# A gated cross-attention block on one core: the whole order of loads and stages replaced

## The reference

```python
x = x + tanh(g_xattn[0]) * fake_quant(layernorm(x)) @ fake_quant(ctx)       # 512 rows of 512, ctx (2, 512, 512)
x = x + tanh(g_ffn[0]) * (layernorm(x) @ W_base.T + b_base + 0.5 * low_rank_update(x))
q, k, v = layernorm(x) @ w_q.T, ctx @ w_k.T, ctx @ w_v.T                    # 32 heads of 16, 8 key/value groups
x = x + tanh(g_xattn[1]) * (softmax(mask(q @ k.T / 4)) @ v) @ w_out.T       # 256 queries, 512 keys, batch 2
h = weight_quant(w_gate), weight_quant(w_up), weight_quant(w_down)          # ternary weights, 1376 hidden
x = x + tanh(g_ffn[1]) * bitlinear(relu(bitlinear(n, w_gate))**2 * bitlinear(n, w_up), w_down)   # n = layernorm(x)
```

## Time and profile before

| what | value |
|---|---|
| median of 3 runs | 261.47 us (261.21 to 261.71) |
| span of the profiled execution | 259.9 us; its own whole time is not given, the runs lie 1.3 to 1.8 us above the span |
| TensorE matmul busy | 244.6 us (94%) |
| VectorE busy | 206.9 us (80%) |
| ScalarE busy | 190.2 us (73%) |
| GpSimd busy | 124.0 us (48%) |
| bytes moved | 27.63 MB |

### The profile page before, as it was taken

The page is one execution under the profiler, slowest core; times in us unless marked ns, Lnnn a source line. Parts: engine busy times, 40 slices in busy tenths (PEclk is TensorE's granted clock), DMA queues, the critical chain, the costliest instruction groups (busy, mean ns, idle before and its releaser), DMA issues.

```text
span 259.9 us, 4692 instructions
## 1 busy us (share of the span) xinstructions
PE 244.6 (94%) x1472; PEld 120.2 (46%) x1472; DVE 206.9 (80%) x592; ACT 190.2 (73%) x317; POOL 124.0 (48%) x176
## 2 busy tenths in 40 slices
PE   8488989799999999999999999999999999998984
PEld 8443449647433343474244365434334244444431
DVE  3789676669898479767999995989888974999995
ACT  3536598659798998587698388998969988546631
POOL 7005920466332207455888662558978987100000
PEclk9959999999999999999999999999999999999999
DMA  6999962660497850004500830720000000000004
GB/s 190 358 372 358 405 267 63 142 132 4 111 316 221 153 161 3 0 1 112 74 0 0 308 140 0 153 32 1 5 0 0 3 0 0 3 1 0 3 0 161
DMA packets 9154, 27.63 MB, mean 106 GB/s; under 512 B 1514, under 2 KB 4122, under 8 KB 7882
## 3 DMA queue, kind: packets, MB, share of 16 engines
q1 hardware_dynamic: 8698, 21.63, 28.9%
q0 software_dynamic: 288, 5.70, 6.3%
q10 hardware_dynamic: 144, 0.00, 0.0%
HBM read 23.87 MB, written 3.41 MB: 105 GB/s over the span
## 4 chain that ended last, share of the span: by engine, by line
PE 71%; DVE 7%; DMA 7%; SPq 6%; ACT 6%; issue 3%; DVEq 0%; ACTq 0%
PE bank L804 12%; PE bank L831 11%; PE bank L782 10%; DMA big<-in_ctxT 7%; PE bank L807 7%; PE bank L854 5%; PE bank L872 5%; PE bank L724 4%; PE bank L714 4%; PE bank L790 4%; PE bank L760 2%; PE bank L839 1%; DVE fs L1317 1%; SPq L470 1%; PE bank L749 1%
## 5 line engine op out<-in xcount | busy, mean ns | idle before, releaser
L1252 DVE CUSTOM_DVE_ANT_0 junk<-bank,maskb 128x512 bf16<-128x512 f32 x128 | 83.8, 687 | 13.5 <-PE bank L782 12.6
L1026 ACT ACTIVATE big<-bank 128x512 f32<-128x512 f32 x128 | 75.1, 596 | 15.1 <-PE bank L804 10.8
L590 POOL TENSOR_TENSOR big<-big,product 128x512 int32<-128x512 int32 x48 | 61.6, 1285 | 33.6 <-ACT big L1026 33.2
L804 PE MATMUL bank<-qst,kst 99*128 99x512 bf16 x128 | 49.0, 383 | 0.2
L782 PE MATMUL bank<-kst,qst 96*128 96x512 bf16 x128 | 47.8, 381 | 0.6 <-DVE mx L1252 0.4
L831 PE MATMUL bank<-big,vp 128*32 128x512 f32 x256 | 30.6, 598 | 0.0
L807 PE MATMUL bank<-ident_b,maskb 128*128 128x512 bf16 x80 | 30.4, 380 | 0.0
L600 POOL TENSOR_TENSOR mx<-mx 128x4 f32<-128x4 f32 x64 | 16.0, 249 | 22.0 <-DVE mx L1252 19.6
L782 PEld LDWEIGHTS bank<-kst,qst 96*128 96x128 bf16 x128 | 12.5, 99 | 21.4 <-issue 11.0
L804 PEld LDWEIGHTS bank<-qst,kst 99*128 99x128 bf16 x128 | 12.4, 97 | 20.6 <-ACT big L1026 7.2
L1009 ACT ACTIVATE qst<-bank 3x512 bf16<-3x512 f32 x32 | 18.9, 590 | 0.9
(11 more groups left out here) (190 smaller groups left out, 413.2 us busy)
## 6 DMA issues: line engine op xcount, KB each, us to landing
...
stage_w<-in_w_gate SPq DMA_DIRECT2D x1, 2752.0 KB, 15.7
stage_w<-in_w_up POOLq DMA_DIRECT2D x1, 2752.0 KB, 14.8
...
```

The costliest lines, as they stand in the source:

```text
L590: nc.gpsimd.tensor_tensor(p, p, keep[:, nt, KEEP_ST.index(i):KEEP_ST.index(i) + 1, :].broadcast_to([P, HG, P]), ALU.mult).then_inc(kept, 1)
L804: i = mm(o[:, :], kst[0:KM, b, g, s * P:(s + 1) * P], qst[0:KM, tile % 2, g * HG:(g + 1) * HG, :], start=True, stop=by_keep(c, s))
L1026: fn(pt[:, c % 4, s, :], o[:, :], ACT.Exp).then_inc(drain(stage), 1)
L1252: v.tensor_tensor_reduce(junk[:, j % 2, :], o[:, :], maskb[:, tb(c // NG)[1], :], 1.0, HIDE, ALU.add, ALU.max, mx[:, c % 3, 0, hh:hh + 1]) ...
```

## The change

`PREPARATION` and `FILL` are both replaced. The same stages are there once each; the rules for `s`, `t`, `m`, `pv` and `oev`, the lags and the code of every stage stay. All later lines move up by five. A piece of the diff, as an example of its form:

```diff
-    ("load_ctx", 3), ("warm", 0, 0, 42), ("load_ctx", 0), ("load_x", 0), ("scalars",), ("load_ctxT", 1),
+    ("fclamp", 0, 0), ("load_wkv",), ("load_x", 1), ("warm", 0, 0, 42), ("warm", 0, 1, 60), ("warm", 0, 4, 10),
...
-    86: [("y1", 1, 1), ("y1", 1, 2), ("y1", 1, 3), ("f1T", 0), ("y1up", 1)], 87: [("ln3", 1, 0)],
...
+    86: [("q", 3, 0), ("q", 3, 1), ("fabs", 2, 0), ("fabs", 2, 1), ("fclamp", 2, 0), ("fclamp", 2, 1), ("qsplit", 3),
+        ("q", 3, 2), ("q", 3, 3), ("y1up", 1), ("y1", 1, 2), ("y1", 1, 3)],
```

More of the change, by code:

```diff
@@ new lines @@
+    ("scalars",), ("products",), ("xstats", 0), ("ln0", 0, 1), ("ln0", 0, 2), ("ln0", 0, 3), ("ln0", 0, 4),
+    ("load_x", 0), ("pick",), ("k", 1, 0), ("k", 1, 1), ("k", 0, 0), ("ln0", 0, 5), ("xstats", 1), ("load_ctx", 0),
+    ("load_ctx", 3), ("cquant", 0), ("load_ctx", 1), ("q1T", 0), ("csum", 0), ("ln0q", 0), ("xstats", 2),
+    ("xstats", 3), ("ln0", 1, 1), ("ln0", 1, 2), ("load_x", 3), ("load_ctx", 2), ("ln0", 1, 3), ("adapters",),
[3 rows of a table added]
+    ("load_ctxT", 1), ("load_mask",), ("load_wT", 2), ("ln1", 0, 5), ("bias", 0), ("load_wT", 3), ("k", 0, 1),
@@ new lines @@
+    ("fabs", 0, 2), ("fabs", 0, 3), ("ln1", 1, 1), ("load_wq",), ("ln1", 1, 2), ("ksplit", 0), ("hT", 0, 2),
+    ("ln1", 1, 3), ("v", 1, 0), ("load_ones",), ("ln1", 1, 4), ("ln1", 1, 5), ("bias", 1), ("cquant", 1), ("q", 0, 0),
+    ("q", 0, 1), ("hT", 1, 1), ("fscale", 0), ("ln0", 3, 5), ("qsplit", 0), ("v", 0, 3), ("fclamp", 0, 1),
+    ("fclamp", 0, 2), ("q", 0, 2), ("q", 0, 3), ("fround", 0, 0), ("fround", 0, 1), ("fround", 0, 2), ("r", 2),
+    ("csum", 1), ("y0", 1, 0), ("y0", 1, 1), ("y0", 1, 2), ("y0", 1, 3), ("ln0q", 3), ("qpick", 0, 0),
@@ L154 @@
+    116: [("hidden", 0, 2), ("f1T", 1)], 118: [("y1", 2, 0)], 120: [("fround", 2, 3)],
+    121: [("fclamp", 2, 2), ("fternary", 2, 1), ("fternary", 2, 2)], 124: [("fternary", 2, 3)], 125: [("fq", 0, 0)],
[17 rows of a table added]
 }
```

42 lines of the change are left out of this document (17 added, 25 removed), and 86 rows, old and new, of tables (FILL, PREPARATION).

## The result

The changed kernel took 264.35 us (median of 4 runs, 263.90 to 265.85), the kernel before 261.59 us (4 runs, 261.21 to 261.90). The ratio is 1.0112, with a 95% interval of 1.0077 to 1.0146. It is slower by 2.8 us, where I had forecast 4.8 us less. The profiled executions have spans of 262.1 and 259.9 us, so the traces hold 2.2 us of it.

What follows compares the result with a forecast made beforehand. Bounds: loads, then VectorE and ScalarE at the start; TensorE, with hidden waits, in the attention; VectorE at the end. Terms -3.7 + 0 - 1.1 = -4.8 us gave a span of 255.1 and a forecast of 256.7 us, range 254.3 to 260.6.

Steps and rivals of the forecast that it cites:

- The start: Before the attention: key stages fill TensorE's idle time, `csum` begins near 15.5 us, tile 0's `y0` comes 0.8 us earlier.
- `y0 1` at 48.4: In the start: `hT 1 1` copied directly behind the second context's conversion, so `y0 1` starts 3.3 us earlier.
- The first maximum comes 3.7 us earlier, near 56.4: VectorE's first score maximum: 3.3 us from `y0 1`, 0.4 us from the shorter chain behind it.
- First maximum to first transposed score: Eleven maxima and `ksplit 1` on VectorE before the transposed scores: 8.1 us, the same after the change.
- Term 2: The attention, from the first transposed score: no change, 0 us, with bounds -3 and +5.
- My count of groups: In the attention's 32 groups, ScalarE or VectorE exceeds TensorE by 10.6 us before and 10.3 after.
- The first rival: The attention takes part back, likeliest at the up weights' load: price 1 to 3 us, 258.5 to 260.9; chance 0.18.
- The rival "slower": In the attention, lumps of stages leave groups without fill, 0.5 us each: 262 to 265 us; chance 0.11.
- Term 3: The end, on VectorE: last `y2up` starts at 255.6 instead of 256.70, -1.1 us; bounds 0 and -1.8.
- the signs: Prediction wrong if `y0 1` starts at 50 or later, attention over 3 us longer, or ScalarE waits on up weights.

Runs made afterwards that it cites:

- Experiments 1: Changed kernel with the GpSimd memset of the value ones (`vones`) back near the start, behind `products`: 262.87 us.
- experiments 2: Changed kernel with the value ones early and `fclamp 0 2`, `fternary 0 2`, `fround 0 3` moved out of the stretch before the first score: 260.09 us.
- Experiment 6: Changed order up to the first transposed score `t 0 0`, all other stages behind it in the order of before: 263.48 us.
- experiment 3: Changed kernel with 80 filler matmuls on ones added on TensorE ahead of `hT 1 2`, where it idles: 264.38 us.
- 7: Order of before up to the first transposed score `t 0 0`, all other stages behind it in the changed order: 264.04 us.
- Experiment 15: Kernel 7 with `y0 2`, `y0up 2`, `ln2 2`, `ln1 3`, `hT 2 2` and `q 2` put back behind their scores of before: 268.17 us.
- experiment 11: Changed kernel with `fround 2 3` moved from step 120 to 126, `fternary 2 2` and `fternary 2 3` from 121 and 124 to 128: 265.64 us.

## Why the prediction was wrong

By its own steps, in the traces of before and after:

- **The start, right.** The key stages stood at 11.7 to 18 us, `csum` at 18.6 instead of the 15.5 to 17.5 given: two transposed blocks were late (waits of 1.77 and 1.41 us) and the key matmuls ran at half the clock. `y0 0` started at 29.6 us, 0.4 earlier than before and not 0.8, and nothing waited for it. (The 2.25 and 1.75 MB of the working are 2.36 and 1.84; their difference, 0.52, is right.)
- **`y0 1` at 48.4, right:** 47.55. The conversion ended at 46.5 (I had 47.4 to 47.6), the copy of `hT` at 47.4. The gate weights were issued 3.0 us sooner, not 1.5.
- **"The first maximum comes 3.7 us earlier, near 56.4", wrong; this is the step that failed.** It came at 60.60, 4.2 us later than predicted. From `y0 1` on it took 13.05 us where I had 8.0; the missing 0.85 us is `y0 1` itself, which was that much earlier than forecast. I carried VectorE's durations over from the earlier trace rows and asked only which instructions stood in the stretch, not what GpSimd did beside them. The new order puts two additions, the memset and a ternary of GpSimd beside the clamp, VectorE's rounding and the norm's steps, which added 4.6 us to VectorE. Experiments 1 and 2 took GpSimd work away and shortened this stretch by 1.7 and 3.9 us, the runs by 1.5 and 4.3 us. I had named the memset and the roundings as a delay for the up weights' issue only.
- **First maximum to first transposed score, taken as the 8.1 us of before:** 9.4. The wait of 4.70 us on TensorE was followed by the lower clock. Experiment 6 shows it as a loss of 1.3 us with the old rest. In experiment 3 it is gone (7.92 us), but the gain is lost again to a held step, so what it costs the changed kernel stays open.
- **Term 2, the attention, 0: wrong in size, 1.0 us behind the first transposed score.** In experiments 2 and 3 it is 2.1 us and with the old start (7) 2.8. My count of groups priced TensorE against ScalarE in each group, with fixed durations. The same thing that it left out at the start is at work here: the added 1.1 us of 2, 3 and 7 arises where a Newton step is held beside GpSimd, and 7 has 0.7 us more at the split queries. The 1.0 us that every kernel with the new rest shows arises by the 40th score, between 68 and 105 us. Experiment 15 shows that the group of stages from step 24 on, taken apart, costs 4 us more.
- **The first rival's up weights:** no. Issued at 64.1, landed 10.6 us later (14.8 before), no wait. The rival "slower" had the right result, but the price that it named, groups left bare by the lumps, is not what the traces show as the main loss.
- **Term 3, -1.1: half of it.** 24.6 us instead of 25.2, -0.6: the four `y2up` stand back to back, three of them beside the last product, as in the forecast:

```profile
256.68 2.94 DVE L1351 SCALAR_TENSOR_TENSOR x<-bank,cst,x 128x512 f32<-128x512 f32 x4
257.16 1.67 PE L886 MATMUL bank<-ternary,stage_w 128*128 128x512 bf16 x7
```

  The split of the product gave 0.4 us where I had 0.6 (from the first to the last `y2up` 2.2 us instead of 2.6). VectorE's chain ahead of them gave 0.2 us instead of 0.5: the first `y2up` starts 22.45 us behind the last `y1up`, 22.65 before.

The sum by what was measured: a span of 255.1 + 4.2 (first maximum) + 1.3 (clock) + 1.0 (attention) + 0.5 (end) = 262.1, the trace's. Of the signs by which I would have known the prediction to be wrong (`y0 1` at 50 or later, an attention over 3 us longer, a wait on the up weights) none appeared: none of them looked at the stretch that failed.

What stays open is which of the moved stages ahead of step 40 makes the 1.0 us that is in every kernel with the new rest. That the held step costs the 1.1 us is read from six traces that agree, and not from an experiment that took GpSimd's addition away. The 2.0 us by which experiment 11's trace is longer are explained only in part.
